# GRU and expert-choice layer on one core: another order of the recurrent matmuls in a step, expert tiles moved behind the loop, a head by long rows, and a spread reload of x

## The chip, the cores and the metric

One core of a Trainium2 chip. The metric is the device time of one execution, in microseconds (us), and its median over several runs. One core has TensorE (PE; its weight loads are listed apart as PEld), VectorE (DVE), ScalarE (ACT), GpSimd (POOL) and SyncE (SP), and 16 DMA engines.

## What is computed

A GRU cell runs over T = 256 steps with B = 16 sequences and D = 512, on x itself. Its states are the tokens of an expert-choice layer with 16 experts, each of which takes its 256 best tokens of 4096; all experts share one 512x512 weight. The result is added to x. All in float32.

```python
def cell(h, x):
    gi = x @ W_ih + b_ih
    gh = h @ W_hh + b_hh
    i_r, i_z, i_n = jnp.split(gi, 3, axis=-1)
    h_r, h_z, h_n = jnp.split(gh, 3, axis=-1)
    r = sigmoid(i_r + h_r); z = sigmoid(i_z + h_z)
    n = jnp.tanh(i_n + r * h_n)
    h_new = (1.0 - z) * n + z * h
    return (h_new, h_new)
...
S = softmax(xf @ router_w + router_b, axis=-1)
G, idx = jax.lax.top_k(S.T, 256)
out = jnp.einsum('ekh,hd->ekd', xf[idx], expert_w) + expert_b
y = jnp.zeros((bs, h)).at[idx.reshape(-1)].add((G[..., None] * out).reshape(-1, h))
return x + y
```

## The kernel before

**Layout.** The 512 columns of a gate are cut in two halves a = 0, 1 and each half over the four 32-column tiles j of the PE array, so that one PSUM bank `gates[q % 2][a]` holds, for one pair q of steps, the four quantities n-input, r, z and n-recurrent of a half. A matmul with 192 columns of a weight fills r, z, n of one j. Four matmuls, one for each j, lie side by side in the array; a float32 matmul is recorded as two instructions, so such a set of four appears as two groups of four instructions. The contraction is cut in four chunks kc.

**One step t** on PE (`step`, L408 on, with `recurrent`, L392 on) has 8 recurrent sets (2 halves by 4 chunks, 16 groups, 64 instructions; line L403), then the input projection of a half of the next pair (`project`, L380 on; 4 sets, 32 instructions; line L388), then from t = FIRST on one unit of the expert layer (`expert`, L430 on; 4 matmuls of 128 columns, 8 instructions; line L442). Every 32 steps a router piece (`router`, L444 on; line L451) comes between. The new state of half 0 gives chunks kc 0 and 1 of the next step, that of half 1 chunks 2 and 3.

**The chain of a half** is tanh of r and z (`tanh_rz`, L306, ACT, waits for `gh_done[a]`), u, v (L564, L568, DVE), tanh of n (L311, ACT), the 32x32 transposes of z and n (L571, L580), and three more DVE operations whose last (L589) writes the state into `tok` and counts `h_ready[a]`. Both halves go through the same two engines in a fixed order: DVE has `take_r(1)` and `add_in(1)` ahead of `new_state(0)`, ACT has `tanh_n(0)` ahead of `tanh_rz(1)`.

The order of the sets in a step is

```python
for a in range(2):
    for kc in range(KH): recurrent(t, a, kc)
pe.wait_ge(h_ready[1], t)
for a in range(2):
    for kc in range(KH, K): recurrent(t, a, kc)
```

with `gh_done[a]` counted by the last set of a half.

**The expert layer** has 32 token tiles of 16 units each. With IN_LOOP = 15, 240 units lie in the loop from step 16 on, one in a step. Behind the loop come the last router piece, SOFTMAX_UNITS = 32 units, and then a search for each expert's threshold: 15 counting rounds and a last count, in which DVE counts, PE sums over the partitions (`sum_counts`, L498) and puts 8 units (ROUND_UNITS) behind each sum, 4 (SHORT_UNITS) in three places. Then DVE forms a mask, PE turns it into one weight a token (L518), and DVE multiplies each tile by it and adds x (L787), from SBUF for the tiles that ACT has evacuated (22 of them) and straight from one of five PSUM banks for the last 10. OUT_ORDER sets the order: the first five PSUM tiles, the 22 evacuated ones, the other five. A bank is preset with the bias by ACT (L318) once its last tile is out. SP and ACT store the tiles in turn (L252, L374).

**x** is loaded twice: by pieces of 128 bytes for the projection (`load_x`, L214, 8 DMAs a tile of 8 steps), and in rows of 2 KB for the sum at the end (L249): tiles 0 to 29 into `xs`, 30 and 31 into the place of W_hh, all of them on SP's queue behind the last `load_x`.

**Head.** SP loads x tile 0 (8 DMAs of 128-byte pieces), W_ih (8 DMAs), the start state (4), W_hh (4), x tile 1, and the rest; ACT loads the two biases by 8 DMAs of 128-byte pieces over all partitions (L294). In step 0 the sets go through by halves.

## Time and profile before

| | us |
|---|---|
| median of 3 runs (1193.01 to 1197.41) | 1195.52 |
| the profiled execution, its own time | 1198.08 |
| its span, first to last instruction | 1196.3 |
| PE busy (matmul) | 1159.9 |
| PE weight loads busy | 965.6 |
| DVE busy | 767.9 |
| ACT busy | 360.9 |
| POOL busy | 6.4 |

The profiled execution took 1.8 us more than its span, and lies 2.6 us above the median. Matmuls overlap each other, and their ends are modelled, so PE's busy time is not time at its peak. In the page's chain of what ended last, PE has 91% of the span, 56% on line L403 and 26% on L388, and DVE has 5%. DMA moved 37.40 MB; 75712 of its 86356 packets are under 512 bytes.

### The profile page before, as it was taken

The page shows a single profiled execution, that of the slowest core. Times are in us where ns is not written, and L with a number is a line of the kernel's source. Part 1 is how long each engine was busy: PE and PEld are TensorE (multiplying, and loading weights), DVE is VectorE, ACT ScalarE, POOL GpSimd, SP SyncE. Part 2 cuts the span into 40 slices and gives each one's busy share as a digit, 9 for nine tenths or more (in the row PEclk, how much of TensorE's full clock was granted, in tenths as well). Part 3 has the DMA queues.
Part 4 walks back from the last instruction along what each step waited for, and adds up shares of the span by engine and source line. Part 5 has one row for each costly group of instructions (what it writes and reads, how often), then busy time and mean ns, then how long its engine had stood idle before and what let it go on. Part 6 is the DMA issues. An engine that isn't in the chain of part 4 may idle for free.

```text
span 1196.3 us, 64639 instructions
## 1 busy us (share of the span) xinstructions
PE 1159.9 (97%) x28983; PEld 965.6 (81%) x28983; DVE 767.9 (64%) x4248; ACT 360.9 (30%) x1367; POOL 6.4 (1%) x28
## 2 busy tenths in 40 slices
PE   5999999999999999999999999999999999899887
PEld 2778888888888888888888888888888888788776
DVE  1666666666666666666666666666666666566886
ACT  1233232333333232333323232333323232232430
POOL 2000000000000000000000000000000000000000
PEclk9999999999999999999999999999999999999999
DMA  8200000000000000000000000000000006400008
GB/s 245 64 7 9 12 13 12 12 13 12 12 7 9 12 12 13 12 12 12 13 7 9 13 13 12 12 13 12 12 10 5 12 12 157 121 4 4 21 29 257
DMA packets 86356, 37.40 MB, mean 31 GB/s; under 512 B 75712, under 2 KB 75712, under 8 KB 86080
## 3 DMA queue, kind: packets, MB, share of 16 engines
q1 hardware_dynamic: 80576, 28.69, 10.4%
q10 hardware_dynamic: 5504, 4.59, 1.4%
q8 instruction: 226, 3.70, 1.3%
q14 instruction: 50, 0.41, 0.1%
HBM read 24.87 MB, written 8.39 MB: 28 GB/s over the span
## 4 chain that ended last, share of the span: by engine, by line
PE 91%; DVE 5%; issue 1%; DMA 1%; SPq 1%; ACT 0%; DVEq 0%
PE gates L403 56%; PE gates L388 26%; PE ffn_ps L442 6%; DVE wih L665 2%; PE gates L442 2%; DMA whh<-in_L_cond_W_hh 1%; PE log_ps L451 1%; DVE u L564 0%; ACT th L306 0%; DVE zT L571 0%; SPq L214 0%; DVE tok L589 0%; DVE z_h L576 0%; DVE nT L580 0%; DVE reached L681 0%
## 5 line engine op out<-in xcount | busy, mean ns | idle before, releaser
L403 PE MATMUL gates<-whh,tok 128*16 128x192 f32 x16384 | 727.6, 329 | 9.8 <-DMA whh<-in_L_cond_W_hh 4.9
L403 PEld LDWEIGHTS gates<-whh,tok 128*16 128x16 f32 x16384 | 563.4, 125 | 111.7 <-DVE tok L589 7.7
L388 PE MATMUL gates<-wih,xT 128*32 128x192 f32 x8192 | 386.2, 329 | 9.1 <-DMA wih<-in_L_cond_W_ih 8.2
L564 DVE SCALAR_TENSOR_TENSOR u<-th,gates 128x64 f32<-128x64 f32 x512 | 112.6, 220 | 341.1 <-ACT th L306 341.1
L388 PEld LDWEIGHTS gates<-wih,xT 128*32 128x32 f32 x8192 | 268.3, 111 | 76.9 <-DVE xT L536 7.7
L306 ACT ACTIVATE th<-gates 128x128 f32<-128x128 f32 x512 | 137.4, 268 | 486.6 <-PE gates L403 486.6
L311 ACT ACTIVATE n_t<-v 128x64 f32<-128x64 f32 x512 | 131.5, 257 | 277.8 <-DVE v L568 277.8
L442 PE MATMUL ffn_ps<-we,tok 128*32 128x128 f32 x2816 | 128.9, 281 | 3.7 <-issue 3.7
L580 DVE STREAM_TRANSPOSE nT<-n_t 128x64 f32<-128x64 f32 x512 | 123.9, 242 | 0.0
L571 DVE STREAM_TRANSPOSE zT<-th 128x64 f32<-128x64 f32 x512 | 122.0, 238 | 0.0
L568 DVE SCALAR_TENSOR_TENSOR v<-u,gates 128x64 f32<-128x64 f32 x512 | 113.2, 221 | 8.8
L589 DVE SCALAR_TENSOR_TENSOR tok<-new_n,z_h 128x32 f32<-128x32 f32 x512 | 110.7, 216 | 8.7
L576 DVE SCALAR_TENSOR_TENSOR z_h<-zT,half_h 128x32 f32<-128x32 f32 x512 | 98.6, 192 | 17.6
L442 PEld LDWEIGHTS ffn_ps<-we,tok 128*32 128x32 f32 x2816 | 90.9, 114 | 20.4 <-issue 4.2
L584 DVE SCALAR_TENSOR_TENSOR new_n<-zT,nT 128x32 f32<-128x32 f32 x512 | 96.6, 189 | 8.8
L302 ACT ACTIVATE gates<-bias 128x256 f32<-128x256 f32 x256 | 86.4, 369 | 3.9 <-DVE bias L544 3.9
L607 DVE TENSOR_SCALAR half_h<-tok 128x64 f32<-128x64 f32 x256 | 56.9, 222 | 8.8
L442 PE MATMUL gates<-we,tok 128*32 128x128 f32 x1280 | 38.4, 274 | 0.4 <-issue 0.3
L536 DVE STREAM_TRANSPOSE xT<-x_in 128x128 f32<-128x128 f32 x128 | 38.6, 303 | 0.0
L442 PEld LDWEIGHTS gates<-we,tok 128*32 128x32 f32 x1280 | 34.4, 110 | 1.4 <-issue 0.9
L665 DVE TENSOR_SCALAR_CACHE_REDUCE wih<-wih,cand 128x512 uint16<-128x512 uint16 x30 | 21.1, 743 | 0.0
L355 ACT ACTIVATE wih<-wih,cand 128x512 uint16<-128x512 uint16 x15 | 10.8, 722 | 18.9 <-DVE cand L692 13.3
(103 smaller groups left out, 135.6 us busy)
## 6 DMA issues: line engine op xcount, KB each, us to landing
x_in<-in_x SPq DMA_DIRECT2D x256, 32.0 KB, 2.3
xs<-in_x SPq DMA_DIRECT2D x30, 256.0 KB, 7.9
out<-tok SPq DMA_DIRECT2D x16, 256.0 KB, 4.9
out<-tok ACTq DMA_DIRECT2D x16, 256.0 KB, 4.8
whh<-in_L_cond_W_hh SPq DMA_DIRECT2D x4, 768.0 KB, 9.8
wih<-in_L_cond_W_ih SPq DMA_DIRECT2D x4, 512.0 KB, 7.5
wih<-in_L_cond_W_ih SPq DMA_DIRECT2D x4, 256.0 KB, 6.7
we<-in_L_ffn_expert_w SPq DMA_DIRECT2D x1, 1024.0 KB, 5.5
```

Of the source, the lines that this page charges most:

```text
L306: nc.scalar.activation(th[a][:, :, :].rearrange("p g c -> p (g c)"), gates[t // S % 2][a][:, R_:HN], ACT.Tanh, scale=0.5).then_inc(th_read ...
L311: nc.scalar.activation(n_t[a][:, :], v[a][:, :], ACT.Tanh).then_inc(n_ready[a], 1)
L388: nc.tensor.matmul(gates[q % 2][a][Q * j:Q * (j + 1), IN:HN].rearrange("b (g k c) -> b g k c", g=G, k=KH), xT[:, n % 2, kc, first:first + ...
L403: mm = nc.tensor.matmul(gates[t // S % 2][a][Q * j:Q * j + rows, R_:GC].rearrange("b (g k c) -> b g k c", g=G, k=KH), columns, by_tile(whh ...
L442: mm = nc.tensor.matmul(bank(n)[Q * j:Q * (j + 1), cols], tile(n)[:, kc * P + Q * j:kc * P + Q * (j + 1)], we[:, kc, cols], start=False, s ...
L564: V.scalar_tensor_tensor(u[a][:, :], th[a][:, 0, :], 1.0, ps[a][:, HN:GC], ALU.add, ALU.mult).then_inc(u_ready[a], 1)
L568: V.scalar_tensor_tensor(v[a][:, :], u[a][:, :], 0.5, ps[a][:, IN:R_], ALU.mult, ALU.add).then_inc(v_ready[a], 1)
L571: V.transpose(zT[a][:, :, :].rearrange("p k q -> p (k q)"), th[a][:, 1, :]).then_inc(zT_ready[a], 1)
L576: V.scalar_tensor_tensor(z_h[a][:, :, :], zT[a][:, :, rows], 1.0, half_h[:, chunks[a], :], ALU.add, ALU.mult)
L580: V.transpose(nT[a][:, :, :].rearrange("p k q -> p (k q)"), n_t[a][:, :]).then_inc(nT_ready[a], 1)
L584: V.scalar_tensor_tensor(new_n[a][:, :, :], zT[a][:, :, rows], 1.0, nT[a][:, :, rows], ALU.subtract, ALU.mult).then_inc(new_n_ready[a], 1)
L589: V.scalar_tensor_tensor(by_chunk[:, chunks[a]], new_n[a][:, :, :], -0.5, z_h[a][:, :, :], ALU.mult, ALU.add).then_inc(h_ready[a], 1)
```

## The change

**Order in a step.** Half 0 gets both its late chunks directly behind the wait for `h_ready[1]`, and only one set of half 1 stands ahead of that wait instead of two. `gh_done[0]` is thus counted behind 5 sets instead of 6, and `h_ready[1]` is waited for behind 3 sets instead of 4. In step 0 the order is by chunks, both halves of a chunk together.

**Expert units.** IN_LOOP is 12, so the units begin at step 64. The last two steps, which have no projection, take 6 units more each, and 2 stand behind the loop ahead of the router. Behind the router come 28 units instead of 32, and a counting round has 9 instead of 8. ACT evacuates 21 tiles, and 11 are read from PSUM; OUT_ORDER has the first five at places 0 to 4 and the other six at places 9, 14, 18, 22, 27 and 31, between the evacuated ones.

**Head.** x tile 0 comes as one DMA of 2 KB rows, and PE turns it by four matmuls against an identity matrix (which POOL makes) into PSUM; DVE copies it to `xT`. The biases come as one row each in 3 DMAs, and 16 matmuls with one row of ones put them straight into `gates[0]`; ACT copies them out as `bias`. The start state is one DMA and four small PE turns. W_ih is loaded in whole rows of 6 KB, 4 DMAs, and DVE copies its n block to the front (four copies of 128x512). PE clears four PSUM banks ahead of this and three behind it.

**Reload of x.** One tile of `xs` follows each `load_x` from tile 2 on, 26 in all; six tiles instead of two go into the place of W_hh behind the loop.

PE in one odd step of the loop's first part, with the waits that stand ahead of a matmul (`h_ready0`, `v_ready1`, `h_ready1`; four rows of matmuls are one set). Before:

```order
L403 MATMUL gates<-whh,tok 32x192 [waits h_ready0]
L403 MATMUL gates<-whh,tok 32x192 x7
L403 MATMUL gates<-whh,tok 32x192 [waits v_ready1]
L403 MATMUL gates<-whh,tok 32x192 x7
L403 MATMUL gates<-whh,tok 32x192 [waits h_ready1]
L403 MATMUL gates<-whh,tok 32x192 x15
```

and with the change:

```order
L427 MATMUL gates<-whh,tok 32x192 [waits h_ready0]
L427 MATMUL gates<-whh,tok 32x192 x7
L427 MATMUL gates<-whh,tok 32x192 [waits v_ready1]
L427 MATMUL gates<-whh,tok 32x192 x3
L427 MATMUL gates<-whh,tok 32x192 [waits h_ready1]
L427 MATMUL gates<-whh,tok 32x192 x19
```

The wait for the state of half 1 now stands behind 12 matmuls instead of 16; 20 follow it.

PE from the last step's late sets to the first unit behind the router. Before:

```order
L403 MATMUL gates<-whh,tok 32x192 [waits h_ready1]
L403 MATMUL gates<-whh,tok 32x192 x15
L442 MATMUL ffn_ps<-we,tok 32x128 x4
L451 MATMUL log_ps<-tok,wr 32x128 [waits h_ready1]
L451 MATMUL log_ps<-tok,wr 32x128 x15
```

and with the change:

```order
L427 MATMUL gates<-whh,tok 32x192 [waits h_ready1]
L427 MATMUL gates<-whh,tok 32x192 x19
L468 MATMUL ffn_ps<-we,tok 32x128 x36
L477 MATMUL log_ps<-tok,wr 32x128 [waits h_ready1]
L477 MATMUL log_ps<-tok,wr 32x128 x15
```

Nine units (36 matmuls) instead of one stand between the last recurrent matmul and the router's wait.

SP's queue around the last loads of x tiles. Before:

```order
L214 DMA x_in<-in_x 16x16x32 [waits xT_ready]
L214 DMA x_in<-in_x 16x16x32 x7
L249 DMA xs<-in_x 128x1x512 x30
L249 DMA whh<-in_x 128x1x512 [waits gh_done1]
L249 DMA whh<-in_x 128x1x512
```

and with the change, where one `xs` load follows a tile and no block stands at the end:

```order
L229 DMA x_in<-in_x 16x16x32 x7
L252 DMA xs<-in_x 128x1x512
L229 DMA x_in<-in_x 16x16x32 [waits xT_ready]
L229 DMA x_in<-in_x 16x16x32 x7
...
L252 DMA whh<-in_x 128x1x512 [waits gh_done1]
L252 DMA whh<-in_x 128x1x512 x5
```

The core of the diff:

```diff
-    XS = 30
+    XS = 26
-    IN_LOOP = 15
+    IN_LOOP = 12
-    SOFTMAX_UNITS, ROUND_UNITS, SHORT_UNITS = 32, 8, 4
-    EVACUATED = 7
+    LAST_UNITS, SOFTMAX_UNITS, ROUND_UNITS, SHORT_UNITS = 6, 28, 9, 4
+    EVACUATED = 9
     IN_PSUM = IN_LOOP + EVACUATED
-    OUT_ORDER = [*range(IN_PSUM, IN_PSUM + BANKS), *range(IN_PSUM), *range(IN_PSUM + BANKS, NT)]
+    PSUM_PLACES = [0, 1, 2, 3, 4, 9, 14, 18, 22, 27, 31]
...
-            load_x(0)
+            sp.dma_start(x_first, x_rows[0]).then_inc(first_loaded, 16)
             for kc in range(K):
-                sp.dma_start(wih[:, kc, 0, :], w_ih[rows, 2 * D:]).then_inc(wih_loaded[kc], 16)
-                sp.dma_start(wih[:, kc, 1:, :].rearrange("p g d -> p (g d)"), w_ih[rows, 0:2 * D]).then_inc(wih_loaded[kc], 16)
...
+                sp.dma_start(wih[:, kc, 1:, :].rearrange("p g d -> p (g d)"),
+                             w_ih[kc * P:(kc + 1) * P, :]).then_inc(wih_loaded[kc], 16)
...
+            for n in range(2, NT):
+                if n >= 3:
+                    sp.wait_ge(xT_ready, (n - 1) * K)
+                load_x(n)
+                if n - 2 < XS:
+                    load_xs(n - 2)
+            sp.wait_ge(gh_done[1], T)
+            for n in range(XS, NT):
+                load_xs(n)
...
+            act.dma_start(bih[:, 0, :], b_ih.rearrange("(o g c) -> o g c", o=1, g=G)[:, 2]).then_inc(b_loaded, 16)
+            act.dma_start(bih[:, 1:, :], b_ih.rearrange("(o g c) -> o g c", o=1, g=G)[:, 0:2]).then_inc(b_loaded, 16)
+            act.dma_start(bhh, b_hh.rearrange("(o g c) -> o g c", o=1, g=G)).then_inc(b_loaded, 16)
+            act.dma_start(h0, cond).then_inc(h0_loaded, 16)
...
+                if t == 0:
+                    for kc in range(K):
+                        pe.wait_ge(whh_loaded[kc], 16)
+                        for a in range(2):
+                            recurrent(t, a, kc)
+                    return
+                for kc in range(KH):
+                    recurrent(t, 0, kc)
+                if t % S == 1:
+                    pe.wait_ge(v_ready[1], t)
+                recurrent(t, 1, 0)
+                pe.wait_ge(h_ready[1], t)
+                for kc in range(KH, K):
+                    recurrent(t, 0, kc)
+                for kc in range(1, K):
+                    recurrent(t, 1, kc)
...
+                else:
+                    expert(LAST_UNITS)
                 if t >= FIRST:
                     expert(1)
+            expert(2)
...
+            for kc in range(K):
+                dve.wait_ge(wih_loaded[kc], 16)
+                V.tensor_copy(wih[:, kc, 0, :], wih[:, kc, G, :]).then_inc(wih_turned, 1)
```

## Rows read from the trace of the kernel before

**Rows 1.** Windows view of the loop: us; PE, PEld, DVE, ACT, POOL busy; PEclk; DMA

```profile
97.70:1013.00 915.30, 915.30 (x22888) 765.58 (x22880) 592.96 (x3375) 284.80 (x1117) 0.00 (x0) 1.00 0.08 15
```

**Rows 2.** Timeline of PE: step with a unit; start us, us, then the instructions

```profile
1087.29 2.84 PE L403 MATMUL gates<-whh,tok 128*32 128x192 f32 x64
1089.94 1.48 PE L388 MATMUL gates<-wih,xT 128*32 128x192 f32 x32
1091.24 0.40 PE L442 MATMUL ffn_ps<-we,tok 128*32 128x128 f32 x8
1091.47 0.37 PE L403 MATMUL gates<-whh,tok 128*16 128x192 f32 x4
```

**Rows 3.** Timeline of PE, first and third of three steps without a unit

```profile
85.30 2.81 PE L403 MATMUL gates<-whh,tok 128*16 128x192 f32 x64
...
93.64 0.37 PE L403 MATMUL gates<-whh,tok 128*16 128x192 f32 x4
```

**Rows 4.** Timeline of ACT and DVE in the step of Rows 2

```profile
1089.54 0.28 ACT L306 ACTIVATE th<-gates 128x128 f32<-128x128 f32 x1 [2.15 <-PE gates L403]
...
1090.52 0.26 ACT L306 ACTIVATE th<-gates 128x128 f32<-128x128 f32 x1
...
1091.21 0.21 DVE L589 SCALAR_TENSOR_TENSOR tok<-new_n,z_h 128x32 f32<-128x32 f32 x1
...
1092.19 0.23 DVE L589 SCALAR_TENSOR_TENSOR tok<-new_n,z_h 128x32 f32<-128x32 f32 x1
```

**Rows 5.** Timeline of SP and PE in the stretch in which xs is loaded

```profile
1008.54 11.97 SPq L249 DMA_DIRECT2D xs<-in_x  x17
...
1015.87 1.69 PE L403 MATMUL gates<-whh,tok 128*32 128x192 f32 x35 [0.60 <-issue]
...
1024.00 1.16 PE L403 MATMUL gates<-whh,tok 128*16 128x192 f32 x11 [2.48 <-issue]
```

**Rows 6.** Chain that ended last, two of its PE rows around that stretch

```profile
1009.75 2.65 PE gates L403 x64
1037.37 2.65 PE gates L403 x64
```

**Rows 7.** Timeline of PE in the head

```profile
17.14 1.51 PE L388 MATMUL gates<-wih,xT 128*32 128x192 f32 x16 [0.55 <-DMA wih<-in_L_cond_W_ih]
...
27.13 2.10 PE L403 MATMUL gates<-whh,tok 128*16 128x192 f32 x24 [3.37 <-DMA whh<-in_L_cond_W_hh]
...
31.10 0.35 PE L403 MATMUL gates<-whh,tok 128*32 128x192 f32 x4
```

**Rows 8.** DMA view, 0 to 8 us; first row: busy tenths in 40 slices

```profile
DMA  0000000004897359735289999999999999999999
...
DMA packets 5386, 0.71 MB, mean 88 GB/s; under 512 B 5361, under 2 KB 5361, under 8 KB 5386
```

**Rows 9.** DMA view, 8.4 to 16 us

```profile
DMA packets 1106, 3.00 MB, mean 395 GB/s; under 512 B 146, under 2 KB 146, under 8 KB 1106
```

**Rows 10.** Timeline of PE and DVE at the loop's end

```profile
1103.99 2.84 PE L403 MATMUL gates<-whh,tok 128*32 128x192 f32 x64 [1.13 <-DVE tok L589]
...
1109.16 1.91 PE L451 MATMUL log_ps<-tok,wr 128*32 128x128 f32 x32 [2.12 <-DVE tok L589]
...
1111.13 0.72 DVE L637 STREAM_TRANSPOSE wih<-log_ps 128x512 f32<-128x512 f32 x1 [1.77 <-PE log_ps L451]
```

**Rows 11.** Timeline of PE in a counting round: units, then the next sum

```profile
1121.18 1.96 PE L442 MATMUL gates<-we,tok 128*32 128x128 f32 x64
1123.32 0.16 PE L498 MATMUL log_ps<-cnt,same_expert 128*128 128x3 f16 x1 [0.19 <-DVE wih L665]
```

**Rows 12.** Timeline of PE and DVE from the weights to the last tile

```profile
1160.94 3.35 PE L442 MATMUL ffn_ps<-we,tok 128*32 128x128 f32 x64
...
1183.16 5.02 PE L442 MATMUL ffn_ps<-we,tok 128*32 128x128 f32 x113 [2.52 <-issue]
...
1191.94 0.75 DVE L787 SCALAR_TENSOR_TENSOR tok<-gates,weight,whh 128x512 f32<-128x512 f32 x1 [2.97 <-PE gates L442]
```

More of the change, by code:

```diff
@@ L49, in gru_expert_choice_kernel @@
     BANKS = 5
-    SOFTMAX_UNITS, ROUND_UNITS, SHORT_UNITS = 32, 8, 4
-    EVACUATED = 7
+    LAST_UNITS, SOFTMAX_UNITS, ROUND_UNITS, SHORT_UNITS = 6, 28, 9, 4
+    EVACUATED = 9
     IN_PSUM = IN_LOOP + EVACUATED
-    OUT_ORDER = [*range(IN_PSUM, IN_PSUM + BANKS), *range(IN_PSUM), *range(IN_PSUM + BANKS, NT)]
+    PSUM_PLACES = [0, 1, 2, 3, 4, 9, 14, 18, 22, 27, 31]
+    stored_tiles, psum_tiles = iter(range(IN_PSUM)), iter(range(IN_PSUM, NT))
+    OUT_ORDER = [next(psum_tiles if i in PSUM_PLACES else stored_tiles) for i in range(NT)]
     FFN_LOADS = (4 + NI) * 16
@@ L103, in tile @@
             return tok[:, PAD + n * D:PAD + (n + 1) * D]
-        h0 = tile(NT - 1)[:, 0:P]
-        h0_t = tile(NT - 1)[:, P:2 * P]
-        b_rows = [tile(NT - 2 - i)[:, 0:G * P] for i in range(2)]
+        x_first = tile(NT - 2)
+        h0 = tile(NT - 3)[0:B, :]
+        h0_t = tile(NT - 1)[:, 0:K * B]
+        ident = tile(NT - 4)[:, 0:P]
+        ones = tile(NT - 4)[0:1, P:P + Q]
+        bih, bhh = (tok[0:1, PAD + n * D:PAD + (n + G) * D].rearrange("p (g c) -> p g c", g=G) for n in (NT - 8, NT - 12))
         xs = sb("xs", [P, XS, D])
@@ L323, in store_ffn @@
                 nc.scalar.activation(tile(n), bank(n)[:, :], ACT.Copy).then_inc(ffn_stored, 1)
-            act.wait_ge(bias_ready, 1)
+            act.wait_ge(bias_summed, 1)
+            for a in range(2):
+                nc.scalar.activation(bias[:, a, :], gates[0][a][:, 0:GC], ACT.Copy).then_inc(bias_ready, 1)
             act.wait_ge(bits_set, 1)
-            set_biases(0)
+            act.wait_ge(bias_ready, 2)
             set_biases(1)
@@ L341, in _ @@
                     store_ffn((t - FIRST) // UNITS - 1)
-                if t >= FIRST and (t - FIRST) % UNITS == 2 and (t - FIRST) // UNITS + 1 < IN_LOOP:
+                if t >= FIRST and (t - FIRST) % UNITS == 2 and (t - FIRST) // UNITS + 1 <= IN_LOOP:
                     preset_ffn((t - FIRST) // UNITS + 1)
-            for n in range(IN_LOOP, IN_LOOP + BANKS - 1):
+            for n in range(IN_LOOP + 1, IN_LOOP + BANKS - 1):
                 preset_ffn(n)
@@ L454, in router, with set_bits @@
                 mm.then_inc(log_done, 1)
[L457 to L459 removed]
+            def set_bits(ps):
                 for j in range(J):
@@ L462, in _ @@
                                           skip_group_check=True)
+                return mm
+            pe.wait_ge(zeros16_ready, 1)
+            for ps in (ffn_ps[0], gates[0][0], gates[0][1], ffn_ps[1]):
+                set_bits(ps)
+            pe.wait_ge(ident_ready, 1)
+            pe.wait_ge(first_loaded, 16)
+            for k in range(K):
+                mm = nc.tensor.matmul(ffn_ps[0][:, k * P:(k + 1) * P], x_first[:, k * P:(k + 1) * P], ident,
+                                      start=False, stop=True, skip_group_check=True)
+            mm.then_inc(x_first_turned, 1)
+            pe.wait_ge(ones_ready, 1)
+            pe.wait_ge(b_loaded, 3 * 16)
+            for a in range(2):
+                for b, first in ((bih, IN), (bhh, R_)):
+                    for j in range(J):
+                        mm = nc.tensor.matmul(gates[0][a][Q * j:Q * (j + 1), first:first + G * HC]
+                                              .rearrange("b (g k c) -> b g k c", g=G, k=KH), ones,
+                                              b[:, :, a * HC * J:(a + 1) * HC * J].rearrange("p g (k j c) -> p j g k c", j=J, c=Q)[:, j],
+                                              start=False, stop=(b is bhh), skip_group_check=True)
+            mm.then_inc(bias_summed, 1)
+            pe.wait_ge(h0_loaded, 16)
+            for k in range(K):
+                mm = nc.tensor.matmul(ffn_ps[1][:, k * B:(k + 1) * B], h0[:, k * P:(k + 1) * P], ident[0:B, 0:B],
+                                      start=False, stop=True, skip_group_check=True)
+            mm.then_inc(h0_turned, 1)
+            for ps in (gates[1][0], gates[1][1], log_ps[:, :, :].rearrange("p g c -> p (g c)")):
+                mm = set_bits(ps)
             mm.then_inc(bits_set, 1)
```

102 lines of the change are left out of this document (39 added, 63 removed).

## The prediction

> **What bounds the kernel now.** I read the table of busy time by stretch first, then the timeline of single steps, then the chain that ended last and the DMA view. In the loop PE is shown busy all the time at a granted clock of 1.00 [rows 1], which looks like a bound. The timeline says otherwise. A step with a unit starts 4.18 us after the one before, 1087.29 to 1091.47 [rows 2]; two steps without a unit take 8.34 (85.30 to 93.64) [rows 3], 4.17 each. The unit costs nothing: something else sets the step. It is the chain of half 0: its first tanh starts 2.25 us behind the step's first matmul, its new state is written 1.88 us later (1089.54 to 1091.21 + 0.21) [rows 4], and 0.05 us behind that the next step starts: 4.18.
>
> PE's own time is less. The 8 groups of a projection take 1.30 us (1089.94 to 1091.24) [rows 2], 0.1625 each. The 24 groups of a step without a unit are then 3.90, and a unit adds two groups of its own kind: 16 of them last 1.96 and 2 last 0.40 [rows 2, 11], so one is 1.56/14 = 0.11, a unit 0.22 and the tail behind the last start 0.29. Together 4.12.
>
> **Order in a step.** `gh_done[0]` is counted two groups earlier, 0.325 us. Three loops have to be checked. Through half 0: 4.18 - 0.33 = 3.85. Through DVE's order, where `take_r(1)` stands ahead of `new_state(0)`: the tanh of half 1 starts at 3.23 behind the step's start [rows 2, 4], but there it stands behind the tanh of n; the last group's data are there near 2.9, so it can move ahead by the same 0.33, and DVE with it. Through half 1: its state is there 1.00 us behind that of half 0 [rows 4], 1.05 with the hop; PE needs it now behind 6 groups, 0.975, where it was 1.30. From there the first tanh follows after 2.25 - 8 x 0.1625 = 0.95, and the second state after 1.88 + 1.00, so this loop takes 0.95 + 2.88 + 0.05 = 3.88. All three lie under PE's 3.90 without a unit, by 0.02 to 0.05, and well under 4.12 with one. So PE becomes the bound. Where the margin is that small, a weight load that starts late is no longer hidden, and I take 3.93. Ends: 3.90, and 4.17, where nothing is gained. With a unit 4.12 (ends 4.10 and 4.18).
>
> Steps 1 to 63 (63 of them) gain 4.175 - 3.93 = 0.245 each, **15.4**. Steps 64 to 253 (190) gain 0.055 each, **10.5**. The router pieces cost the same in both. What was free in 48 steps of the loop, the units, is now paid for or hidden elsewhere: 14 of the 48 fill gaps in the last two steps, 15 are added to the rounds, the rest comes behind the weights (below).
>
> **Reload of x.** The block of 30 loads makes PE wait for its own instructions ("issue", 0.60 and 2.48, and one more) [rows 5]. Two sets that lie five steps apart in the chain start 27.62 us apart [rows 6]; five steps are 20.9, so the block costs 6.7. Spread, each 256 KB load is over long before the next; in the block the first stall came over 6 us behind its first DMA (1008.54 to 1015.3) [rows 5], and one such load, 0.26 MB, is under 1 us at the head's rate [rows 9]. I take **6.6** gained. Ends: 0 if the stalls merely spread, 6.7. The six late loads (four more than before) run in the softmax stretch, 5 to 6 us of full DMA, at the edge of that same time: at nothing, with an end of +2.5, one stall as above.
>
> **Head.** Up to 8 us DMA moves 0.71 MB, nearly all in packets under 512 bytes, at 88 GB/s [rows 8]; then W_ih flows at 395 GB/s [rows 9]. With long rows x tile 0, W_ih and W_hh are 6.55 MB, 16.6 us from 1.8, where DMA starts [rows 8], and the last W_ih was used about 1 us behind its data (3.15 MB from 8 us on, used at 17.14) [rows 7, 9]: last W_hh used at 19.5 instead of 27.13. Behind it the same 3.97 us to step 1 (27.13 to 31.10) [rows 7]: 23.5, **7.6** gained. By the Trainium skill ("DMA: Bandwidth & Descriptors", Why small descriptors are slow) one core gets at most about 358 GB/s from HBM; this trace shows 395. By the page's figure the last W_hh would come about 2 us later and the result would be 1156; I go by the row. The turns on PE, the bias and the copies of the n block have to be done by then: W_ih chunks land every 2 us, a DVE pass over 128x512 takes 0.75 [rows 12], so they hide behind the loads. If the last piece lags, as before (3.37 of waiting, where the other pieces came 2 apart), 2 us of this go.
>
> **End of the loop.** From the last step's start to the router is 5.17 and to DVE's first operation on the logits 7.14 [rows 10]. The last step's second state comes 1.93 + 1.88 + 1.00 + 0.05 = 4.86 behind its start; PE has 16 groups and 9 units till then, 2.60 + 1.98 = 4.58. The router's 8 groups last 1.91 there, where 8 x 0.11 and the tail make 1.17: PE had just stood idle for 1.13 and 2.12 [rows 10], which I take for the cause; with the gap filled I take 1.17: 6.0, **1.1** gained (0.4 if they are as slow anyway).
>
> **Rounds.** Units end and the next sum starts 2.14 us behind their start; 8 of them last 1.96 with the tail, and PE then waits 0.19 for DVE's count [rows 11]. A ninth, 0.22, takes that wait and little more. Zero; ends 0 and +1.5 (0.1 in each of 15).
>
> **Behind the weights.** Of the 512 units 408 were done by the weights, 104 were left: 22.9 us at 0.22, but PE needs 1160.94 to 1191.9, so 8 us went into waits for instructions under the stores (2.52 and smaller) and into a slower pace behind them (5.02 for 28 groups, where 28 x 0.11 and the tail make 3.4) [rows 12]. Now 206 + 28 + 67 + 67 + 4 + 13 = 385 are done, 127 are left, 27.9 us. The stores are paced by PE: 3 or 4 evacuated tiles between two from PSUM, each of which takes PE 3.5, instead of 22 in a row, so they queue less, and I take 3 of the 8 us for stalls: 30.9, the same as before, **0**. Ends: -3 (no stalls), +5 (all of them).
>
> **Sum.** 15.4 + 10.5 + 6.6 + 7.6 + 1.1 = 41.2 us. The span goes from 1196.3 to 1155.1. Its own time was 1198.1, 2.6 above the median of the runs, which gives 1156.9 for an execution like it; against the median, 1195.5 - 41.2 = 1154.3, so **1154**.
>
> **The rivals.**
> 1. *PE is already full.* Then the step is PE's busy time: with a unit 4.18 stays, without one 4.18 - 0.22 = 3.96, and the time is 1154 + 10.5 + 1.9 = 1167. For it: the busy row [rows 1]. Against it: steps without a unit are no shorter [rows 3]. "Trainium Kernel Development and Optimization" in the Trainium skill (Reading a trace) calls matmul busy time a bad measure and goes by the weight loads; here these are at 84%, so the trace sides with it. 0.08.
> 2. *The chain does not follow.* Something I have not seen (ACT's order, DVE's order) holds half 0 at 4.17: the order gains nothing, the 26 us of the steps are lost, 1180. Against it: each piece of the chain starts with its releaser in the rows. 0.07.
> 3. *The reload spreads its stalls.* Each of 26 loads costs PE one short stall of 0.6 as the first of the block [rows 5]: +15.6, 1170. Against it: the first loads of the block, 6 us of them, cost nothing. 0.06.
> 4. *Slower.* The wait for `h_ready[1]` is met 0.325 earlier. If the state of half 1 came so late that its loop took over 4.24 instead of 3.88, each of 254 steps would lose 0.18 and more against my mean, 47 us, and the time would be over 1201. It decides from 0.36 us more between a first tanh and the second state than the 2.88 of [rows 4]; the same operations run in the same order, so I see no source for it. 0.02.
>
> **Chances.** The forecast 0.73, the four rivals 0.23, and 0.04 for things not named, such as a PE that stays slow behind the new head. The range: low end all favourable bounds, 1154 - 3 (stores) - 2 (3.90) - 2 (head); high end rival 1 or the adverse bounds of head, late loads, rounds and stores together (2 + 2.5 + 1.5 + 5), 1147 to 1168. It leaves out rivals 2 to 4. A measurement of this kernel can tell no less than 0.5%, 6 us, from no change; all cases but the last are faster by more. Faster 0.97, same 0.01, slower 0.02.
>
> **What would show it.** Step starts 3.93 apart before step 64 and 4.12 behind; the first tanh 1.92 behind a step's start; no idle "issue" near 1010; the last W_hh used near 19.5; the router 4.9 behind the last step's start; PE some 31 us from weights to end. I am wrong if steps without a unit stay above 4.0, or if "issue" waits show in the loop or grow at the end.

## The result, and the profile after

The changed kernel takes 1159.92 us (median of 4 runs, 1159.66 to 1161.92) against 1195.38 for the kernel before: a ratio of 0.970, 95% interval 0.9685 to 0.9721, 35.5 us. On a second chip it was 1161.58 (5 runs) against 1194.29, ratio 0.973 (0.9717 to 0.9749). The forecast was 1154, range 1147 to 1168. Its own time in the profiled execution is 1161.92, its span 1159.3. The other executions of that series had spans of 1157.1 to 1157.5. What a time has beyond its span is 2.6 us in the profiled execution, where it was 1.8 before.

The page of the changed kernel: engines, and the chain of what ended last.

```profile
PE 1140.0 (98%) x29031; PEld 962.5 (83%) x29031; DVE 770.7 (66%) x4245; ACT 362.9 (31%) x1366; POOL 6.8 (1%) x31
...
PE 95%; DVE 2%; DMA 1%; issue 1%; SPq 0%; ACT 0%; DVEq 0%
PE gates L427 57%; PE gates L412 29%; PE ffn_ps L468 5%; PE gates L468 3%; DMA whh<-in_L_cond_W_hh 1%; PE log_ps L477 1%; DVE wih L713 1%; SPq L234 0%; PE log_ps L550 0%; SPq L237 0%; DVE thr_upper L734 0%; DVE reached L729 0%; PE gates L570 0%; DVE wih L760 0%; DVE wih L791 0%
```

PE's share of the chain has gone from 91% to 95%, that of DVE from 5% to 2%: the loop follows PE. The steps, against [rows 2, 3, 4]; timeline of PE, two steps without a unit, then two with one, and the ACT and DVE rows of half 0 and half 1 in the step that starts at 1051.71 (start us, us, instructions):

```profile
84.15 2.78 PE L427 MATMUL gates<-whh,tok 128*16 128x192 f32 x64
...
88.05 2.78 PE L427 MATMUL gates<-whh,tok 128*32 128x192 f32 x64
...
91.95 0.34 PE L427 MATMUL gates<-whh,tok 128*16 128x192 f32 x4
...
1051.71 2.78 PE L427 MATMUL gates<-whh,tok 128*16 128x192 f32 x64
...
1055.82 2.78 PE L427 MATMUL gates<-whh,tok 128*32 128x192 f32 x64
```

```profile
1053.58 0.28 ACT L324 ACTIVATE th<-gates 128x128 f32<-128x128 f32 x1 [1.49 <-PE gates L427]
...
1055.26 0.21 DVE L637 SCALAR_TENSOR_TENSOR tok<-new_n,z_h 128x32 f32<-128x32 f32 x1
1056.24 0.22 DVE L637 SCALAR_TENSOR_TENSOR tok<-new_n,z_h 128x32 f32<-128x32 f32 x1
```

A step without a unit is 3.90 us, with one 4.11 to 4.12. The new state of half 0 is there at 1055.47, 0.35 before PE begins the next step, where it was 0.05 before. The first tanh starts 1.87 us behind the step's start (1.92 was forecast). The state of half 1 is there at 1056.46, and PE wants it 6 groups (0.975) behind 1055.82, at 1056.80. Without a unit both margins are some 0.13. PE has no idle time named "issue" anywhere between 30 and 1064 us. The window of [rows 1], taken from the changed kernel:

```profile
97.70:1013.00 915.30, 915.30 (x23080) 773.44 (x23076) 609.43 (x3458) 291.78 (x1140) 0.00 (x0) 1.00 0.09 18
```

PE is busy all the time here too, and its weight loads are busy for 84.5% of it (773.44 of 915.30), against 84% before. Neither share tells whether PE or the chain sets the step; the step starts with and without a unit do.

The head, against [rows 7], and two windows of it (us; busy of PE, PEld, DVE, ACT, POOL; PEclk; DMA share; GB/s):

```profile
16.14 1.47 PE L427 MATMUL gates<-whh,tok 128*16 128x192 f32 x32
19.28 0.84 PE L427 MATMUL gates<-whh,tok 128*16 128x192 f32 x16 [1.67 <-DMA whh<-in_L_cond_W_hh]
22.28 1.48 PE L427 MATMUL gates<-whh,tok 128*16 128x192 f32 x16 [2.15 <-DMA whh<-in_L_cond_W_hh]
...
25.63 1.64 PE L427 MATMUL gates<-whh,tok 128*32 128x192 f32 x36
```

```profile
4.00:6.00 2.00, 1.55 (x7) 1.58 (x8) 0.00 (x0) 0.00 (x1) 1.43 (x5) 1.00 1.03 400
...
18.00:20.00 2.00, 0.72 (x16) 0.37 (x16) 0.00 (x0) 0.00 (x0) 0.00 (x0) 1.00 1.27 252
...
22.00:24.00 2.00, 1.72 (x24) 1.03 (x28) 0.47 (x3) 0.28 (x1) 0.00 (x0) 0.50 0.41 44
```

The long rows flow at 400 to 429 GB/s from 4 to 16 us. Then the rate falls to 252, the last piece of W_hh is used at 22.28, 3.0 us behind the one before it, and PE's clock is at half behind that wait. Step 1 starts at 25.63 instead of 31.10.

From the weights to the end, against [rows 12]: timeline of PE, then of DVE, then the window at 1120.

```profile
1118.71 1.06 PE L570 MATMUL gates<-group_of,wih 128*128 128x8 f32 x8 [1.27 <-DVE wih L820]
1119.69 8.64 PE L468 MATMUL gates<-we,tok 128*32 128x128 f32 x248
1128.15 6.29 PE L468 MATMUL ffn_ps<-we,tok 128*32 128x128 f32 x223
1135.28 1.14 PE L468 MATMUL ffn_ps<-we,tok 128*32 128x128 f32 x33 [0.84 <-issue]
1136.18 2.80 PE L468 MATMUL gates<-we,tok 128*32 128x128 f32 x95
1140.67 3.70 PE L468 MATMUL gates<-we,tok 128*32 128x128 f32 x128 [1.69 <-issue]
1144.69 3.70 PE L468 MATMUL gates<-we,tok 128*32 128x128 f32 x128 [0.32 <-issue]
1148.99 1.14 PE L468 MATMUL gates<-we,tok 128*32 128x128 f32 x33 [0.59 <-issue]
...
1154.10 1.14 PE L468 MATMUL ffn_ps<-we,tok 128*32 128x128 f32 x33 [1.42 <-issue]
```

```profile
1155.28 0.75 DVE L835 SCALAR_TENSOR_TENSOR tok<-ffn_ps,weight,whh 128x512 f32<-128x512 f32 x1 [2.38 <-PE ffn_ps L468]
```

```profile
1120.00:1124.00 4.00, 4.00 (x99) 4.00 (x93) 2.07 (x3) 1.80 (x3) 0.00 (x0) 0.60 0.47 138
```

PE needs 35.5 us (1119.69 to 1155.2) for 127 units. 4.9 us of it are five waits named "issue", always 128 matmuls apart (33 + 95, 128, 128, 33 + 95 in the rows; 223 stands for 224, a record is missing). The 248 matmuls ahead of them were slow under a granted clock of 0.60, most of these 4 us at 1.2 instead of 2.4 GHz.

**The budget of the profiled execution.** The span is 4.2 us over the 1155.1 of the sum:

| stretch | before | after | gained | forecast |
|---|---|---|---|---|
| start to step 1 | 31.10 | 25.63 | 5.5 | 7.6 |
| step 1 to step 255 | 1072.9 | 1038.4 | 34.5 | 32.5 |
| last step to DVE's first logits operation | 7.14 | 5.96 | 1.2 | 1.1 |
| from there to the copy of the weights | 49.9 | 49.8 | 0.1 | 0 |
| the copy of the weights to the end | 35.3 | 39.5 | -4.2 | 0 |

### The profile page after: what moved, and what is told of

It is laid out like the page before. It is cut to its first block, busy times and chain, and to the rows that moved or that the text cites. A ratio compares the mean times of both kernels' runs of the same rounds, so it can differ in the third digit from the quotient of the medians.

```text
span 1159.3 us, 64715 instructions
## 1 busy us (share of the span) xinstructions
PE 1140.0 (98%) x29031; PEld 962.5 (83%) x29031; DVE 770.7 (66%) x4245; ACT 362.9 (31%) x1366; POOL 6.8 (1%) x31
## 4 chain that ended last, share of the span: by engine, by line
PE 95%; DVE 2%; DMA 1%; issue 1%; SPq 0%; ACT 0%; DVEq 0%
PE gates L427 57%; PE gates L412 29%; PE ffn_ps L468 5%; PE gates L468 3%; DMA whh<-in_L_cond_W_hh 1%; PE log_ps L477 1%; DVE wih L713 1%; SPq L234 0%; PE log_ps L550 0%; SPq L237 0%; DVE thr_upper L734 0%; DVE reached L729 0%; PE gates L570 0%; DVE wih L760 0%; DVE wih L791 0%
## 5 line engine op out<-in xcount | busy, mean ns | idle before, releaser
L427 PE MATMUL gates<-whh,tok 128*16 128x192 f32 x16384 | 713.2, 326 | 3.8 <-DMA whh<-in_L_cond_W_hh 3.8
L412 PE MATMUL gates<-wih,xT 128*32 128x192 f32 x8192 | 381.3, 327 | 0.0
L412 PEld LDWEIGHTS gates<-wih,xT 128*32 128x32 f32 x8192 | 264.1, 111 | 67.5 <-issue 0.4
L468 PE MATMUL ffn_ps<-we,tok 128*32 128x128 f32 x2560 | 108.0, 273 | 2.3 <-issue 2.3
L468 PEld LDWEIGHTS ffn_ps<-we,tok 128*32 128x32 f32 x2560 | 77.3, 110 | 16.0 <-issue 2.9
L468 PE MATMUL gates<-we,tok 128*32 128x128 f32 x1536 | 47.4, 280 | 2.6 <-issue 2.6
L468 PEld LDWEIGHTS gates<-we,tok 128*32 128x32 f32 x1536 | 43.1, 113 | 3.7 <-issue 3.4
```

The source lines that it names most:

```text
L412: nc.tensor.matmul(gates[q % 2][a][Q * j:Q * (j + 1), IN:HN].rearrange("b (g k c) -> b g k c", g=G, k=KH), xT[:, n % 2, kc, first:first + ...
L427: mm = nc.tensor.matmul(gates[t // S % 2][a][Q * j:Q * j + rows, R_:GC].rearrange("b (g k c) -> b g k c", g=G, k=KH), columns, by_tile(whh ...
L468: mm = nc.tensor.matmul(bank(n)[Q * j:Q * (j + 1), cols], tile(n)[:, kc * P + Q * j:kc * P + Q * (j + 1)], we[:, kc, cols], start=False, s ...
```

## The experiments

Eleven variants and a second run of the changed kernel, each beside runs of the kernel before on the same chip. Medians from different series differ by 1 to 2 us for the same kernel, so small differences are read from the traces.

### 1. The order of the recurrent groups, alone

The kernel before, with this in the steps from 1 on; step 0 has the order by chunks of the changed kernel besides:

```
-                for a in range(2):
-                    ...
-                        recurrent(t, a, kc)
+                for kc in range(KH):
+                    recurrent(t, 0, kc)
+                ...
+                recurrent(t, 1, 0)
+                pe.wait_ge(h_ready[1], t)
+                for kc in range(KH, K):
+                    recurrent(t, 0, kc)
+                for kc in range(1, K):
+                    recurrent(t, 1, kc)
```

> The kernel before with nothing but the new order of the recurrent groups (15 tiles of the expert layer still in the loop). Theory (the chain of half 0 set the step, the order shortens it below PE's own time): steps 1 to 15, without a unit, start 3.90 us apart instead of 4.17, steps 16 to 254, with one, 4.12 instead of 4.18. Gain 15 x 0.27 + 238 x 0.06 = 18 us, time 1177 to 1178. Rival (the order does nothing by itself, the loop got shorter because units left it): steps stay at 4.17 and 4.18, time 1195. Rival (PE already full): 3.96 and 4.18, time 1192.

Measured: 1175.98 us against 1196.25, ratio 0.984 (0.9804 to 0.9869). The trace, a step with a unit:

```profile
500.08 2.78 PE L403 MATMUL gates<-whh,tok 128*32 128x192 f32 x64
...
504.20 2.12 PE L403 MATMUL gates<-whh,tok 128*16 128x192 f32 x47
```

Steps with a unit are 4.12, those without 3.90, from step 2 on. Step 1 was 4.72. Step 1 to step 255 takes 1056.4 us instead of 1072.9: 16.5 gained. Both rivals fall. The medians differ by 20.3 us, the profiled spans by 22.2 (1196.3 and 1174.1): 16.5 in the loop, 1.1 from the last step to the first logits operation, 1.1 in the head and the search together, and 3.5 behind the weights (31.8 against 35.3), where both kernels have the same instructions. So the part behind the weights differs by some us between executions of the same instructions.

### 2. The old order in the changed kernel

The same edit reversed in the changed kernel, from step 1 on; step 0 stays as changed.

> The changed kernel with the old order of the recurrent groups, all else as changed. Theory: every step is the chain's again, 4.17 to 4.18 with and without a unit; loss 63 x 0.27 + 190 x 0.06 = 28 us, time 1188. Rival (units leaving the loop are what shortened it): steps without a unit stay at 3.90 to 3.96, loss at most 190 x 0.06 + 63 x 0.06 = 15 us, time 1175 or less.

Measured: 1188.17 us (1196.25 before, ratio 0.993, 0.9908 to 0.9957). Timeline of PE, steps without a unit:

```profile
96.63 2.81 PE L427 MATMUL gates<-whh,tok 128*16 128x192 f32 x64
...
100.78 2.84 PE L427 MATMUL gates<-whh,tok 128*32 128x192 f32 x64
...
104.97 0.37 PE L427 MATMUL gates<-whh,tok 128*16 128x192 f32 x4
```

4.15 and 4.19, and with a unit 4.13 to 4.20: taking units out of steps is worth nothing while the chain sets them. From step 1 to step 255 it is 1066.0 instead of 1038.4. So the order is worth 27.5 us here, but only 16.5 in experiment 1: the order and the emptied steps are worth more together than the one alone.

### 3. The spread reload, alone

The kernel before, with `load_xs(n - 2)` behind each `load_x(n)` in place of the block of 30.

> The kernel before with nothing but the reload of x spread over the loop (one 256 KB load with each x tile). Theory: the block's stalls of PE near 1010 to 1030 vanish and none comes in their place; gain 6.6 us, time 1188.7. Rival (the stalls merely spread, a load costs some 0.2 us wherever it stands): time 1195, steps near each load longer. No other part of the trace should move by more than 0.5 us.

Measured: 1189.96 us, ratio 0.995 (0.9932 to 0.9964), 6.3 us. Step 1 to step 255: 1066.3 instead of 1072.9, 6.6 us, with every step from 2 on at its usual 4.13 to 4.20, but for those with a router piece. The loads spread cost nothing.

The 6.7 us that the block cost were not all waits. PE waited 4.0 us (0.60, 2.48 and 0.96), and behind the wait of 2.48 it ran for a while at half clock. Window of the kernel before:

```profile
1024.00:1028.00 4.00, 4.00 (x64) 3.04 (x67) 1.93 (x11) 0.54 (x2) 0.00 (x0) 0.58 1.06 271
```

### 4. x tile 1 behind W_hh

The changed kernel with one wait on SP:

```
+            sp.wait_ge(whh_loaded[K - 1], 16)
             load_x(1)
```

> The changed kernel, where the load of x tile 1 (128-byte pieces) waits until the last piece of W_hh has landed. Theory (those pieces, which start at 18.5 us, slow the last W_hh piece): the last piece is used at about 20.5 instead of 22.28, step 1 starts at about 23.8 instead of 25.63, time 1158. Rival (a last piece is late by itself, its completion comes 1.5 us behind its last packet whatever else runs): used at 22 again, time 1160. Rival (x tile 1 now comes too late for DVE's turn in step 2): a wait in DVE and PE of 1 us or more near 32, time 1160 to 1163.

Measured: 1158.90 us, ratio 0.969 (0.9658 to 0.9719). Timeline of PE in the head, and the wait on it between 30 and 44 us (us in total, times, longest):

```profile
19.11 0.84 PE L428 MATMUL gates<-whh,tok 128*16 128x192 f32 x16 [2.12 <-DMA whh<-in_L_cond_W_hh]
20.96 1.48 PE L428 MATMUL gates<-whh,tok 128*16 128x192 f32 x16 [1.00 <-DMA whh<-in_L_cond_W_hh]
...
24.33 1.96 PE L428 MATMUL gates<-whh,tok 128*32 128x192 f32 x44
```

```profile
PE gates L413 <- issue: 0.3, 1, 0.3
```

The last piece is used 1.3 us earlier and step 1 starts 1.3 earlier. The same holds in the other traces: with this wait (here and in experiments 11 and 12) the last piece is used at 20.91 to 20.96, in the seven traces of the changed head without it at 21.95 to 22.28. So the 2048 packets of 128 bytes of x tile 1, which began at 18.5 us, had held up the last 768 KB by 1.0 to 1.3 us. The piece is still late, though x tile 1 now waits for it. GB/s row of the DMA view of 15 to 24 us (40 slices of 0.225 us):

```profile
GB/s 437 437 455 355 382 410 382 410 382 410 437 410 437 410 382 410 246 137 27 27 27 27 27 27 0 0 0 0 0 0 25 158 41 80 51 39 42 44 24 6
```

From 19.05 to 20.4 us the rest of W_hh comes at 27 GB/s, while under a tenth of the 16 engines' time is used. Why the rest lies with so few of them no run shows.

Half of the 1.3 us is lost again: step 4 takes 4.40 us, with a wait for instructions in it, while the 1 MB of expert weights lands at 306 GB/s. It looks like the stall of the reload block again, in small; it came in this execution and not in experiment 11, which loads in the same way. Neither rival had foreseen it. The medians can't tell 1 us.

### 5. The five tiles from PSUM first, the 21 evacuated ones in a row

```
-    PSUM_PLACES = [0, 1, 2, 3, 4, 9, 14, 18, 22, 27, 31]
+    PSUM_PLACES = [0, 1, 2, 3, 4, 26, 27, 28, 29, 30, 31]
```

> The changed kernel with the tiles that are read from PSUM grouped as before: five first, then the 21 evacuated ones in a row, then the last six. Theory (stores in a row starve PE's instruction fetch, spread stores less): the stalls of PE named issue behind the weights grow from 4.9 us to 8 us or more, and the time by 3 to 5 us, 1163 to 1165. Rival (the order of the output tiles does not matter, PE's remaining 127 units and the memory traffic in sum do): within 1 us of 1160.

Measured: 1161.99 us (1195.83 before, ratio 0.974, 0.9708 to 0.9767). "Issue" waits behind the weights: 0.57, 1.69, 1.97 and 0.60, 4.8 us in sum, as in the changed kernel (4.9), not 8. The rival holds by the waits; the time is 2 us above its 1160, but the changed kernel itself had 1159.92 on one chip and 1161.58 on another. By itself the order of the output tiles did not matter. The stretch at half clock was missing this time: window 1120 to 1124 of this kernel, whose instructions are the same up to there, behind the same idle 1.28 us:

```profile
1120.00:1124.00 4.00, 4.00 (x157) 4.00 (x149) 2.82 (x5) 1.81 (x3) 0.00 (x0) 1.00 0.47 137
```

and the first 248 matmuls took 7.26 us instead of 8.64.

### 6. Only 8 of the 32 tiles stored

> The changed kernel that stores only 8 of its 32 output tiles (every fourth; the other 24 stay in SBUF, so three quarters of the output are left unwritten). It tells what the stores cost PE. Theory (PE's issue stalls behind the weights come from the stores filling the DMA queues): the stalls vanish, PE needs 127 x 0.22 = 28 us and about 1.5 us for the half-clock stretch, 30 instead of 35.5; time 1154.5. Rival (the stalls belong to PE's own instruction stream or to waits for banks): PE still needs 34 us or more, time 1158 or more.

Measured: 1158.40 us (ratio 0.970, 0.9676 to 0.9732). Timeline of PE behind the weights:

```profile
1118.77 8.64 PE L468 MATMUL gates<-we,tok 128*32 128x128 f32 x248
...
1133.68 1.14 PE L468 MATMUL ffn_ps<-we,tok 128*32 128x128 f32 x33 [0.16 <-issue]
...
1138.24 8.63 PE L468 MATMUL gates<-we,tok 128*32 128x128 f32 x289 [0.87 <-issue]
...
1150.30 1.14 PE L468 MATMUL ffn_ps<-we,tok 128*32 128x128 f32 x33 [0.87 <-issue]
```

PE needs 32.7 us instead of 35.5. The stores make 3 of the 4.9 us, and 1.9 stay although DMA moves only 58 GB/s on average (1128 to 1152). PE's time lies between theory and rival, the time as a whole where the rival had it, and it gave the next theory, for what is left sits at the same places in the program.

What comes at these places shows in the trace's record of single DMA packets: on queue q8, whose kind is "instruction", one packet of 16,384 bytes comes for each 128 matmuls with their weight loads.

| kernel | packet starts, ends (us) | PE resumes | behind the packet's end |
|---|---|---|---|
| changed | 1132.82, 1133.86 | 1135.28 | 1.42 |
| changed | 1138.30, 1139.26 | 1140.67 | 1.41 |
| changed | 1142.09, 1143.28 | 1144.69 | 1.41 |
| changed | 1151.78, 1152.66 | 1154.10 | 1.44 |
| experiment 6 | 1135.83, 1136.79 | 1138.24 | 1.45 |
| before, in the reload block [rows 5] | 1013.12, 1014.37 | 1015.87 | 1.50 |
| before, in the reload block [rows 5] | 1021.28, 1022.55 | 1024.00 | 1.45 |

The table has seven of them; from 30 us on, every wait named "issue" of 0.15 us and more in the traces of the two kernels and of experiments 1 to 8 and 10 ends 1.2 to 1.6 us behind the end of such a packet. Between PE's return from one wait and the start of the next packet there are 1.2 and 2.2 us with few stores (1138.24 to 1139.43 in experiment 6 is the shorter) and up to 3.0 with all in the changed kernel (1135.28 to 1138.30). That the block is asked for when PE returns is an assumption, no trace shows the request. By it, with 1.0 for the packet and 1.4 behind it, a block takes 3.6 to 5.4 us to arrive, and PE has worked it off in 3.5. In a loop step 128 matmuls last 5.2 us (32 groups of 0.1625), which is why nothing shows there until a burst of loads comes.

The Trainium skill ("Runtime: NRT & Kernel Launch", Instruction fetch mechanics) says that each engine's instructions are refilled in blocks of 16 KiB, 256 instructions, and that crossing into the next block is mostly hidden. The trace agrees with the block. It does not agree that it is hidden where PE uses one up in 3.5 us.

### 7. PE's two idle stretches filled

33 instead of 28 units in the softmax stretch, 19 instead of 13 ahead of the sums of the weights.

> The changed kernel with 5 more units in the softmax stretch (33 instead of 28) and 6 more ahead of the weight sums (19 instead of 13), to fill the two stretches in which PE stood idle (1.30 us before the first count, 1.27 us before the sums of the weights). Theory 1 (that idle is what drops the granted clock to 0.60 behind it): the two gaps close, the clock stays at 1.0 from 1118 on, PE has 116 units left, and the time falls by 2.4 us for the units and about 1.5 us for the clock, 1156. Theory 2 (the clock falls for another reason): 0.60 stays, time 1157.5. Rival (the end is paced by the stores, not by PE): 1160.

Measured: 1158.22 us, ratio 0.970 (0.9673 to 0.9732), and 3.8 us under experiment 5 of the same series. Both gaps are closed, the clock is 1.00 from 1116 on. From the weights PE needs 31.0 us, of which 4.4 are "issue" waits. The span is 2.0 under the second run of the changed kernel (below), which had a full clock too; the 11 units are 2.4 by the sum. As that run and experiment 5 had the full clock with the idle stretch still there, this one doesn't show that filling it keeps the clock up. The rival, 1160, falls.

### 8. The changed kernel again

> The changed kernel once more, on the chip on which the next two run, so that differences of a few us can be told. Theory (the stretch at half clock behind the sums of the weights, 1120 to 1124, comes in some executions only): the clock there may be 1.0 this time, and PE's span from the weights to the end then 34 instead of 35.5 us; the time 1158 to 1161. Rival (the stretch belongs to the kernel): 0.60 again.

Measured: 1161.58 us (1194.29 before). The idle 1.27 ahead of the sums is there again, and the window behind it reads:

```profile
1120.00:1124.00 4.00, 4.00 (x134) 3.98 (x137) 2.36 (x5) 1.81 (x3) 0.00 (x0) 1.00 0.26 63
```

So the half clock at this place comes in some executions only. From the weights PE needed 32.9 us, with 3.8 of "issue".

### 9. Matmuls of 512 columns behind the weights

A quarter of the instructions for the same sums:

```
+                    if wide and quarter == 0 and unit + 4 <= end:
+                        cols = slice(0, D)
+                        ...
+                        for j in range(J):
+                            mm = nc.tensor.matmul(bank(n)[Q * j:Q * (j + 1), cols], ..., we[:, kc, cols], ...)
+                        ...
+                        unit += 4
+                        continue
...
-            expert(NT * UNITS)
+            expert(NT * UNITS, wide=True)
```

> The changed kernel, where behind the weights a group of four units is issued as 4 matmuls of 512 columns instead of 16 of 128: the same sums in the same order, a quarter of the instructions. Theory (each stall of PE named issue is a block of 128 matmuls with their weight loads, one 16 KB instruction packet on queue q8, that is asked for too late: PE resumes 1.4 us behind the end of such a packet each time): the blocks now last four times as long, no issue stall is left behind the weights, PE needs 127 x 0.22 = 28 us and the half clock where it comes, and the time falls by 4 to 5 us, 1155 to 1156. Rival (PE is slowed by the stores themselves, SBUF or memory traffic, not by its instructions): stalls or slower groups remain, time within 1.5 us of the changed kernel's. Rival (512 columns take longer than four times 128): the pace of a tile rises above 3.52 us.

Measured: 1155.15 us, ratio 0.968 (0.9662 to 0.9694), 6.4 us under the changed kernel (1161.58) on the same chip. The profiled spans differ by 6.0 (1157.5 and 1151.5), of which 4.9 lie behind the copy of the weights. Timeline of PE, then the fifth tile on DVE, then the GB/s row and two queues of the DMA view of 1119 to 1152 us (slices of 0.825 us):

```profile
1120.11 6.19 PE L470 MATMUL gates<-we,tok 128*32 128x512 f32 x56
...
1132.98 10.48 PE L470 MATMUL gates<-we,tok 128*32 128x512 f32 x96
1143.28 3.62 PE L470 MATMUL ffn_ps<-we,tok 128*32 128x512 f32 x32
```

```profile
1126.37 0.75 DVE L847 SCALAR_TENSOR_TENSOR tok<-gates,weight,xs 128x512 f32<-128x512 f32 x1 [2.68 <-PE gates L470]
```

```profile
GB/s 0 0 0 107 308 363 196 141 169 7 10 127 340 365 276 266 318 348 340 328 328 363 372 365 333 330 367 330 320 313 355 370 363 367 365 325 328 273 45 0
q1 hardware_dynamic: 2304, 4.20, 39.4%
q8 instruction: 2, 0.03, 0.4%
```

No matmul waits any more; two instruction packets instead of seven; a tile takes 3.43 us; PE needs 27.5 us (1119.43 to 1146.9). Both rivals fall. That all stores still run at up to 372 GB/s beside PE shows that they slowed it through its instructions alone.

### 10. The same in the kernel before

> The kernel before with matmuls of 512 columns behind the weights, nothing else changed. Theory (there too PE's waits for its instructions, 8 us by the prediction's count, set the end): PE needs 104 x 0.22 = 23 us from the weights instead of 31, the stalls are gone, and the time falls by 6 to 8 us to 1187 or 1189, unless the stores (8.4 MB at 345 GB/s are 24.3 us, and they start some 2 us behind the weights) then set it, which allows 6 us. Rival (the kernel before was paced by its stores already): less than 2 us gained.

Measured: 1193.61 us (12 runs) against 1195.32 (17 runs), ratio 0.999 (0.9974 to 1.0). Timeline of DVE, the fifth and the last tile, and the GB/s row of the DMA view of 1160 to 1194 us (40 slices of 0.85 us):

```profile
1168.42 0.75 DVE L799 SCALAR_TENSOR_TENSOR tok<-gates,weight,xs 128x512 f32<-128x512 f32 x1 [2.68 <-PE gates L444]
...
1186.30 0.74 DVE L799 SCALAR_TENSOR_TENSOR tok<-gates,weight,whh 128x512 f32<-128x512 f32 x1
```

```profile
GB/s 0 0 0 0 89 296 357 183 145 164 0 29 145 352 349 268 251 328 337 342 308 325 359 381 335 362 354 349 352 374 352 349 359 359 359 345 354 268 41 0
```

PE's stalls are gone and the last tile is computed 5.6 us earlier than in [rows 12] (1186.30 for 1191.94), yet the end comes at 1193.8. Up to 1171 PE fed the stores one tile at a time, and they moved little. Then 22 tiles came at once, and from 1172 on the stores run without a break, at 320 to 380 GB/s for most of it, up to 1192. The rival holds: in the kernel before, the stores stood right behind PE.

The same edit gave 6.4 us in the changed kernel, and the traces show no part of the order of the tiles in that. In both orders the first five tiles come straight from PSUM, at PE's pace, and the fifth starts 6.8 to 6.9 us behind the copy of the weights (1126.37 and 1168.42 in the rows). From there to the end, for the other 28 tiles, it is

| kernel | order of the PSUM tiles | matmuls behind the weights | fifth tile to end (us) |
|---|---|---|---|
| experiment 9 | spread | 512 columns | 25.1 |
| experiments 11, 12 | spread | 512 columns | 25.4, 25.2 |
| experiment 10 | grouped | 512 columns | 25.4 |
| before, experiments 1, 3 | grouped | 128 columns | 28.5, 26.4, 26.8 |
| changed, its second run, experiment 7 | spread | 128 columns | 30.9, 29.9, 30.4 |
| experiment 5 | grouped | 128 columns | 30.9 |

With 512 columns the stretch is the same in either order, with the stores running nearly without a break in both GB/s rows. With 128 columns the kernel before was 1 to 3 us above that, and the changed one, which has six tiles to compute in this stretch and not five, some 5. That is what the edit could give back. The changed kernel with 512 columns and the grouped order was not run.

### 11. All together

x tile 1 behind W_hh, the gaps filled, and 512 columns from the softmax stretch on.

> The candidate to beat both: the changed kernel with x tile 1 behind W_hh, the two idle stretches of PE filled (33 units in the softmax, 19 ahead of the sums of the weights) and matmuls of 512 columns from the softmax stretch on. Theory: 0.6 us from the head, 2.5 us from the gaps, 5 us from the stalls: 8 us under the changed kernel, 1152. Rival (behind the weights DVE, 32 passes of 0.75, or the stores, 8.4 MB at 340 GB/s or 24.7 us, bind once PE does not): 1154 or more, PE waiting for banks.

Measured: 1150.15 us, ratio 0.963 (0.9618 to 0.9649), 11.4 us under the changed kernel on the same chip, more than the sum of 8: experiment 9 alone gave 6.4. The profiled spans differ by 9.0 (1157.5 and 1148.5): 7.0 behind the weights, 2.0 in the head and the loop. The rival (1154 or more) falls.

### 12. The expert weights in four pieces besides

The kernel of experiment 11, whose label is e9, with this load spread; DVE's wait for these weights moves from step 8 to step 30.

> The combined kernel (e9) with the expert weights loaded in four pieces of 256 KB, one with each of x tiles 2 to 5, instead of in one piece of 1 MB right behind the head. Theory (that burst, 306 GB/s from 34 to 38 us, delays one instruction packet and gives PE a stall of 0.6 us in step 4): no step between 1 and 30 is over 3.93 us, the stretch from step 1 to step 255 is 0.7 us shorter, time 0.7 us under e9, which the trace can tell and the timing hardly. Rival (the stall belongs to x tile 2 or to the packet's place in the program): it stays.

Measured: 1150.23 us, ratio 0.962 (0.9607 to 0.9636). Steps 2 to 15 are 3.90 but for step 3 (3.93). The stall of 0.5 us in step 4 of experiment 4 (4.40) had not come in experiment 11 either (3.90); there only steps 5 to 7 were longer, 3.99, 3.94 and 3.93, and these are 3.90 now. Step 1 to step 255 takes 1038.5 us, against 1038.7 in experiment 11 and 1039.1 in experiment 4. So the spread load was worth 0.2 us and not 0.7, no time can tell it, and that the burst had made the stall of experiment 4 is not shown. A window behind the weights:

```profile
1136.00:1140.00 4.00, 4.00 (x40) 1.17 (x36) 3.96 (x7) 0.00 (x0) 0.00 (x0) 1.00 1.02 343
```

PE, DVE (99% of this window, 86 and 78% of the two ahead of it) and the stores (343 to 346 GB/s) are now all near full at the end.

## Why the prediction was right, and where it was off

**Direction, size and range** held, by the mechanism named: the chain of half 0 set the step. Rival 1 (PE full) falls with 3.90 without a unit, rival 2 (the chain doesn't follow) with the two steps above, rival 3 (stalls spread) with experiment 3, rival 4 with the margin of 0.34 at `h_ready[1]`.

**Steps.** Forecast 3.93 and 4.12; 3.90 and 4.12 came. The 0.03 that I had added for late weight loads was not needed: 63 x 0.03 = 1.9, all of the error in the loop. That PE's weight loads were busy for 84% was taken as a sign against rival 1; it was none, for they are at 84.5% where PE does set the step. The steps without a unit were the sign that held.

**Reload.** 6.6 forecast, 6.6 in experiment 3. The cost was read as waits for instructions; 4.0 of it were; part of the rest came with the half clock behind the longest wait (above). The six late loads cost nothing that can be told: 49.8 us from the first logits operation to the weights, 49.9 before, 49.5 to 50.2 in the variants.

**End of the loop.** 1.2 for 1.1, but the reason given is not shown, and the size is in part luck. Experiment 1 fills no gap there: PE stands idle for 0.79 and 1.81 us, and yet the router's groups last 1.08 and the stretch is 6.03, 1.1 shorter too. Of that, 0.3 comes from the order (the router starts 4.88 behind the last step instead of 5.17) and 0.8 from the groups, 1.08 instead of 1.91, which in the profiled execution of the kernel before ran at a lower clock (0.66 from 1108 to 1112).

**Rounds.** 0.1 for 0, nine units fit.

**Head: the term of 7.6 measured 5.5.** The step "last W_hh used at 19.5" failed: it was 22.28, 2.8 later, of which 0.6 came back because step 1 follows 3.35 us behind it and not 3.97. Two things in it were wrong. Full rate was reached at 4 us and not at 1.8, though the rate was then higher than the 395 taken (400 to 429). And the last piece lagged, as the text had named as a possibility and left out: x tile 1's short packets made 1.0 to 1.3 us of it, and without them the piece is still used only near 20.9 (experiment 4). The Trainium skill ("DMA: Bandwidth & Descriptors", Measured) has 425 GB/s for one core that loads 16 MB alone, and about 358 where two cores share the memory. This trace, of one core, agrees with the first. The 358 of the prediction stands on that page under Where 436 GB/s comes from, not in the section that it names.

**Behind the weights: the term of 0 measured -4.2, inside its end of +5.** The step that failed is "they queue less, and I take 3 of the 8 us for stalls: 30.9". The waits were 4.9 us (4.0 in the kernel before, 0.32, 1.14 and 2.52), and the order in which the stores come does not set them (experiment 5): a block of 128 matmuls arrives too late for its 3.5 us even with a quarter of the stores (experiment 6), and more units mean more blocks. The stretch at half clock came on top, 1.4 us of the profiled execution, not of all. And the 8 us of the kernel before were no reserve: in part they were half clock, behind the wait of 2.52, which I had put down as a slower pace, and behind the idle ahead of the weight sums (the windows 1184 to 1188 and 1160 to 1164 of the kernel before have 0.57). In experiment 1 the same instructions took 31.8 us to the end and not 35.3. Experiment 10 shows that with PE's waits removed the stores hold the end.

These two, less the loop's 1.9, are the 4 us between sum and span. 0.8 more lies outside the span (2.6 us of the profiled time, where 1.8 was taken over). The median misses the forecast by 5.9 us; that it does not miss by more is in part luck, for the loop's error went the other way.

## What to carry to other kernels

A PE that is "100% busy" in steps of constant length with or without extra work is not the bound, and the share of its weight loads does not tell either: subtract the extra work, and look at which group counts the semaphore that the chain starts from. A chain that gets shorter and filler that is taken out pay only together. Where PE waits for nothing in the profile, compare the waits with the packets of its instruction queue, and try larger instructions (512 columns for 4 x 128): behind the weights they gave 4.9 us in the trace, where another order of the stores gave none. In the loop it was the spreading of the loads that gave 6.6.
